# Scatters one a slot, the output projection ahead of the values, and the router slots' copy of the values moved to VectorE

## The chip, the cores and the metric

The kernel runs on one core of one Trainium2 chip. The metric is the device time of one execution, in microseconds (us). The kernel before has a median of 2207.32 us in three runs (2202.14 to 2223.04).

## The reference

The program computes four transformer layers on 32 sequences of 128 tokens with 256 features, in float32, each with a context of the same shape. Layer 0 projects queries, keys and values head by head, attends to the context with a key mask, and ends in a ReLU feed-forward. Layer 1 is a cross-attention with residual and layer norm. The next layer has a causal self-attention, a cross-attention, and a mixture of experts: a router picks 2 of 8 experts for each token. The last layer attends within a window, gates its result and normalises it. All attentions have 16 heads of 16 features:

```
scores = jnp.einsum('bqhd,bkhd->bhqk', Q, Kp) / jnp.sqrt(jnp.float32(HD))
a = jax.nn.softmax(scores, axis=-1)
o = jnp.einsum('bhqk,bkhd->bqhd', a, V).reshape(Bq, Sq, Dm)
return o @ wo + bo
...
topw, topi = jax.lax.top_k(router_weights, K)
h = jax.nn.gelu(jnp.einsum('td,edf->etf', xf, w1) + b1[:, None, :], approximate=False)
out = jnp.einsum('etd,te->td', eo, combine)
```

## The kernel before, in words

The program is written engine by engine, with semaphores between engines; each engine works through its own list in order. It has three phases. The first does the four attentions ahead of the experts, 128 of them, the second runs the experts over 72 tiles of 128 sorted tokens, the third does the last attention with its gate. The change touches the first phase alone.

The first phase is a chain of slots. A slot is one attention of one sequence. Four sequences go through layer 0, then the same four through layers 1, 2 and 3 (2 is the causal self-attention, 3 the cross-attention of the expert layer), so an iteration has 16 slots, numbered 0 to 15, with layer = slot // 4. There are 8 iterations. The first and the last are written out, the six between are one hardware loop on every engine, and their instructions carry register arithmetic for semaphore counts. `at_(d)` names the slot d places after the present one: `now` is d = 0, `prev` -1, `ff` -2, `rk_` -3, `nxt` +1, `nn` +2.

What each engine does in a slot of the light kind (slots 7 to 15 and 0 to 2; in slots 3 to 6 the feed-forward of layer 0 is mixed in):

- TensorE: scores of `now` (L861, in layer 2 with the mask's L828 ahead), keys and queries of `nxt` (L775, L809), the product of probabilities and values of `prev` (`av`, L926), the transposed maxima of `now` (L913), the transpose of the input of `nn` (L714, L729), the scores again, transposed and exact (`scores_t`, L881 and L888), the values of `nxt` (`values`, L793, or L787 for layer 0), and the output projection of `prev` (`wo`, L939). In slots 14, 15, 0 and 1, the router slots here, a transpose for the router (`fxt`, L714) ends the slot.
- VectorE: layer norm's statistics of `ff` (L1579 to L1584), row maxima of `now` (`mb`, L1557), the output of `prev` divided and transposed (`normalise`, L1567 to L1574, result `oT`), the low parts of queries and keys of `nxt` (`qk_lo`, L1542 or L1545), and the sum of projection and residual of `prev` (`yb`, L1719). In slot 2 it also copies the values of `nxt` from PSUM (`vz`, L1529), ahead of `qk_lo`.
- ScalarE: normalised rows (L1316), queries and keys out of PSUM (L1289, L1292), the transposed maxima (`mT`, L1296), the transposed inputs (L1274), four exponentials (`pt_all`, L1303), then the copy of the values (`vz`, L1375).
- GpSimd: root of the variance (L2030), scaled residuals (L2042, L2044), the queries expanded by heads (`expand`, L2007), then in slots 7 to 10 the scatter of a finished sequence's rows into the experts' order (L2050), then `expand_lo` (L2014).

An iteration's scatters are two indirect DMAs a sequence, one for each chosen expert. They go out in the next iteration: `routed(at_, 8 + s)` is true for sequence s in slot 7 + s. The positions they need are computed by VectorE in slot 6.

## Time and profile before

| what | us |
| --- | --- |
| median of three runs | 2207.32 |
| fastest and slowest run | 2202.14, 2223.04 |
| profiled execution | 2205.66 |
| its span in the trace | 2201.1 |
| TensorE busy | 1972.7 (90%) |
| VectorE busy | 1437.2 (65%) |
| ScalarE busy | 1219.0 (55%) |
| GpSimd busy | 1080.9 (49%) |

The first phase takes about 1340 us of the span. No engine is busy all the time in a slot, so the busy shares don't say what a slot waits for. The chain of waits and the timeline of single slots do.

### The profile page before, as it was taken

The numbers are of one execution on the slowest core, as the hardware profiler recorded it, in microseconds if no ns is written. First come the engines' busy times: TensorE is split into PE (matmuls) and PEld (weight loads), VectorE is DVE, ScalarE is ACT, GpSimd is POOL, SyncE is SP. The second block draws the span as 40 slices with busy tenths as digits, with TensorE's granted clock in tenths as the row PEclk, the third lists the DMA queues.
The fourth block names the chain that finished last, engine by engine and source line by source line (L and its number), as shares of the span: only waits on it lengthen the run. The fifth ranks groups of instructions, "written<-read, shape, count | busy, mean of one in ns | idle before, by whom it ended". The sixth has DMA issues, their size and how long they took to land.

```text
span 2201.1 us, 73195 instructions
## 1 busy us (share of the span) xinstructions
PE 1972.7 (90%) x26048; PEld 1667.3 (76%) x26049; DVE 1437.2 (65%) x3384; ACT 1219.0 (55%) x3083; POOL 1080.9 (49%) x1592
## 2 busy tenths in 40 slices
PE   5999988988988988988988995999999997799997
PEld 4877776866876876776876874899999997677775
DVE  3577676676676676676676685444544543688886
ACT  3366465465465465455455463566556553567775
POOL 3355464464465464465465474322222100788884
PEclk9999999999999999999999996999999998899999
DMA  8501001001001001001000041311112111222220
GB/s 188 183 2 39 8 22 39 8 22 39 8 21 39 8 21 39 8 21 39 8 21 22 2 136 51 117 57 60 59 58 60 38 41 50 62 70 69 68 67 26
DMA packets 97250, 104.38 MB, mean 47 GB/s; under 512 B 23936, under 2 KB 88192, under 8 KB 96896
## 3 DMA queue, kind: packets, MB, share of 16 engines
q1 hardware_dynamic: 87936, 75.96, 11.4%
q0 software_dynamic: 8704, 25.19, 3.7%
q8 instruction: 167, 2.74, 0.5%
q14 instruction: 59, 0.48, 0.1%
q10 hardware_dynamic: 384, 0.01, 0.0%
HBM read 64.68 MB, written 36.44 MB: 46 GB/s over the span
## 4 chain that ended last, share of the span: by engine, by line
PE 64%; DVE 15%; issue 10%; ACT 5%; POOL 3%; DVEq 0%; DMA 0%; ACTq 0%; POOLq 0%; another core or an unknown queue 0%; SPq 0%
PE ps_scores L1137 11%; PE ps_w L1150 9%; DVE mb L1557 8%; PE ps_scores L881 6%; PE ps_w L939 5%; PE ps_xv L714 4%; PE ps_xv L793 4%; PE ps_qk L809 3%; PE ps_qk L960 3%; PE ps_xv L960 3%; PE ps_o L926 2%; ACT pt_all L1303 2%; DVE st L1579 2%; PE ps_scores L888 2%; PE ps_qk L804 1%
## 5 line engine op out<-in xcount | busy, mean ns | idle before, releaser
L1557 DVE TENSOR_REDUCE mb<-ps_scores 128x16 bf16<-128x2048 f32 x160 | 365.6, 2285 | 67.0 <-PE ps_scores L861 66.6
L1303 ACT ACTIVATE pt_all<-ps_scores 128x512 f32<-128x512 f32 x512 | 264.4, 603 | 52.6 <-PE ps_scores L888 47.9
L2030 POOL TENSOR_TENSOR rstd<-ve,neghalf 128x1 f32<-128x1 f32 x192 | 106.8, 556 | 348.0 <-DVE ve L1583 331.7
L1137 PEld LDWEIGHTS ps_scores<-tiles,w_now 128*128 128x128 f32 x2272 | 267.2, 193 | 4.8 <-issue 1.8
L1137 PE MATMUL ps_scores<-tiles,w_now 128*128 128x128 f32 x2272 | 267.8, 277 | 1.2 <-DVE tiles L1850 1.2
L1401 ACT ACTIVATE tiles<-ps_scores,b1s 128x128 f32<-128x128 f32 x568 | 154.6, 384 | 198.0 <-PE ps_scores L1137 182.7
L1150 PE MATMUL ps_w<-w_split,g_split 128*128 x1136 | 219.3, 346 | 5.7 <-DVE g_split L1869 5.7
L2007 POOL TENSOR_TENSOR qbd_all<-qT,consts 128x512 fp32r<-128x512 f32 x160 | 166.4, 1040 | 94.5 <-ACT kT L1289 85.1
L2014 POOL TENSOR_TENSOR lower<-lower,consts 128x512 fp32r<-128x512 f32 x160 | 166.7, 1042 | 86.2 <-DVE lower L1545 43.3
L1150 PEld LDWEIGHTS ps_w<-w_split,g_split 128*128 128x128 f32 x1136 | 174.8, 190 | 30.5 <-issue 6.4
L1316 ACT ACTIVATE xn<-yb,nb,rstd 128x256 f32<-128x256 f32 x160 | 96.3, 602 | 180.9 <-POOL nb L2037 178.9
L926 PE MATMUL ps_o<-pt_all,vz 128*32 128x128 f32 x5120 | 179.8, 282 | 1.3 <-DVE arena L1707 0.8
L926 PEld LDWEIGHTS ps_o<-pt_all,vz 128*32 128x32 f32 x5120 | 134.4, 112 | 25.0 <-issue 14.5
L1860 DVE TENSOR_TENSOR tiles<-ps_w,tiles 128x256 f32<-128x256 f32 x71 | 30.2, 425 | 186.9 <-PE ps_w L1150 186.9
L1719 DVE TENSOR_TENSOR yb<-ps_w,xr 128x256 f32<-128x256 f32 x128 | 54.2, 424 | 141.2 <-PE ps_w L939 140.3
L1393 ACT COPY w_now<-w_experts 128x2048 f32 x72 | 140.2, 1948 | 9.9 <-issue 9.9
L2142 POOL DMA_INDIRECT arena<-sorted_y,pidx x64 | 63.7, 995 | 165.7 <-DMA sorted_y<-tiles 150.4
L2120 POOL CAST w_split<-w_raw 128x256 fp32r<-128x256 f32 x64 | 24.1, 421 | 243.8 <-DVE g_split L1869 238.6
L1274 ACT ACTIVATE xT<-ps_xv,cols_all 128x128 f32<-128x128 f32 x256 | 103.8, 457 | 59.2 <-PE ps_xv L714 58.5
L939 PE MATMUL ps_w<-arena,oT 128*128 128x256 f32 x512 | 133.7, 384 | 2.1 <-DVE oT L1574 2.1
L1567 DVE STREAM_TRANSPOSE ps_o<-ps_o 128x512 f32<-128x512 f32 x160 | 116.1, 725 | 21.6 <-PE ps_o L926 19.9
L714 PE MATMUL ps_xv<-consts,xn 128*128 128x128 f32 x384 | 80.6, 292 | 51.3 <-ACT vz L1375 15.1
(254 smaller groups left out, 4777.8 us busy)
## 6 DMA issues: line engine op xcount, KB each, us to landing
tiles<-sorted_x SPq DMA_DIRECT2D x72, 128.0 KB, 2.0
sorted_y<-tiles SPq DMA_DIRECT2D x71, 128.0 KB, 1.7
w_experts<-in_L_xattn_e_w SPq DMA_DIRECT2D x8, 1024.0 KB, 10.3
w_raw<-in_L_xattn_e_w POOLq DMA_DIRECT2D x8, 1024.0 KB
sorted_x<-zeros SPq DMA_DIRECT2D x8, 640.0 KB
ct_scratch<-cT SPq DMA_DIRECT2D x32, 128.0 KB, 1.7
x_scratch<-x2b_all SPq DMA_DIRECT2D x32, 128.0 KB, 1.7
arena<-x_scratch SPq DMA_DIRECT2D x32, 128.0 KB
```

What stands on the lines that cost most here:

```text
L714: last = nc.tensor.transpose(ps[:, P * c:P * (c + 1)], src[:, P * c:P * (c + 1)], ident)
L881: mm(ps_s[:, g, PAIR * P * c:PAIR * P * (c + 1)], k_[at_strip, kc, :].bitcast(F32R), q_[at_strip, c].rearrange("p e q -> p (e q)").bitcast ...
L926: last = mm(ps_o[32 * q:32 * q + 32, 2 * par + c, :], vz[p][:, h].rearrange("p a d -> p (a d)"), pt[:, SLOTS * q + PAIR * c + par, :], sta ...
L939: last = mm(ps_w[:, 0:D], oT[:, c, :], w[:, c, :], start=c == 0, stop=c == KC - 1)
L1137: last = mm(ps_s[:, 2 * par + j // 4, P * (j % 4):P * (j % 4 + 1)], w1_now[:, par, c, P * j:P * (j + 1)], xgT[par][:, c, :], start=c == 0, ...
L1150: return mm(ps_w[:, 0:n], g_split[:, g_, j, :].bitcast(F32R), w2_split[:, bass.ds(odd * (2 * FC * D) + j * 2 * D, n)].bitcast(F32R), start ...
L1303: nc.scalar.activation(pt[:, 4 * g:4 * g + 4, :].rearrange("p h q -> p (h q)"), ps_s[:, g, :], ACT.Exp, bias=bias, scale=LAYER[l]["scale"] ...
L1393: nc.scalar.copy(w1_now[:, par].rearrange("p c n -> p (c n)"), w1f[:, bass.ds(e * (KC * FF), KC * FF)]).then_inc(w1_copied, 1)
L1401: last = nc.scalar.activation(gT[:, j, :], ps_s[:, 2 * par + j // 4, P * (j % 4):P * (j % 4 + 1)], ACT.Gelu, bias=b1s[par][:, j:j + 1])
L1557: V.tensor_reduce(mb[:].rearrange("p (g r) -> p g r", g=BANKS)[:, :, 0:SLOTS], ps_s[:].rearrange("p g (h k) -> p g h k", h=SLOTS), AX_X, A ...
L2007: G.tensor_tensor(qbd[p].bitcast(F32R), qT[:].unsqueeze(2).to_broadcast([P, KC, PAIR, P]), hmask.unsqueeze(1).unsqueeze(3).to_broadcast([P ...
L2014: G.tensor_tensor(qbd_lo.bitcast(F32R), qT_lo.unsqueeze(2).to_broadcast([P, KC, PAIR, P]), hmask.unsqueeze(1).unsqueeze(3).to_broadcast([P ...
```

## The change

Three edits, all in the first phase.

1. TensorE: in light slots other than slot 2 `wo(prev)` is issued ahead of `values(nxt)` instead of behind it.
2. The copy of the values of `nxt` out of PSUM moves from ScalarE, where it stands behind the exponentials, to VectorE, where it stands ahead of `qk_lo`, in slots 14, 15, 0 and 1.
3. GpSimd: the eight scatters of an iteration go out one a slot in slots 6 to 13, instead of two a slot in slots 7 to 10. In the tail behind the last iteration they stay two a slot.

```diff
@@ TensorE, light slots
                 if now["ok"]:
                     scores_t(now)
+
+                wo_last = ff["ok"] and ff["l"] == 0
+                if prev["ok"] and not wo_last:
+                    wo(prev, first and tau - 1 == 0, w_free)
                 if nxt["ok"]:
...
                     values(nxt, nn["t"] + 1 if nn["ok"] and nn["l"] != 1 else nxt["t"] + 1)
-                if prev["ok"]:
+                if prev["ok"] and wo_last:
                     wo(prev, first and tau - 1 == 0, w_free)
@@ ScalarE
-                if nxt["ok"] and not ff_now:
+                if nxt["ok"] and not (ff["ok"] and ff["l"] in (0, LAYERS - 1)):
                     wait(act, v_psum, nxt["t"] + 1)
@@ VectorE
                 if nxt["ok"]:
-                    if ff["ok"] and ff["l"] == 0:
+                    if ff["ok"] and ff["l"] in (0, LAYERS - 1):
                         vz_evac(nxt)
@@ GpSimd
-        def scatter(n, s):
+        def scatter(n, s, choices=range(TOPK)):
...
-            for k_ in range(TOPK):
+            for k_ in choices:
...
-            for s in range(NS):
-                if routed(at_, 8 + s):
-                    if last and tau == TPI + 8 - 1:
-                        pool.wait_ge(tail_zeroed, 16 * E)
-                    scatter(routed(at_, 8 + s), s)
+
+            if last and tau >= TPI:
+                for s in range(NS):
+                    if routed(at_, 8 + s):
+                        if s == 0:
+                            pool.wait_ge(tail_zeroed, 16 * E)
+                        scatter(routed(at_, 8 + s), s)
+            else:
+                for i_ in range(NS * TOPK):
+                    if routed(at_, 7 + i_):
+                        scatter(routed(at_, 7 + i_), i_ // TOPK, (i_ % TOPK,))
```

The order of VectorE's instructions in slot 14 of the loop (a router slot), from the row maxima of that slot to those of the next. Before:

```order
L1557 TENSOR_REDUCE mb<-ps_scores 128x4x4
L1567 STREAM_TRANSPOSE ps_o<-ps_o 128x512
L1569 RECIPROCAL o_inv<-ps_o 128x16
L1571 TENSOR_TENSOR route_all<-ps_o,o_inv 128x2x8x16
L1574 STREAM_TRANSPOSE oT<-route_all 128x256
L99 REGISTER_ALU
L1545 SCALAR_TENSOR_TENSOR lower<-ps_qk,cols_all,qT 128x128 x2
L1545 SCALAR_TENSOR_TENSOR lower<-ps_qk,cols_all,kT 128x128 x2
L99 REGISTER_ALU
L1719 TENSOR_TENSOR yb<-ps_w,xr 128x256
```

With the change (its line numbers are 4 higher):

```order
L1561 TENSOR_REDUCE mb<-ps_scores 128x4x4
L1571 STREAM_TRANSPOSE ps_o<-ps_o 128x512
L1573 RECIPROCAL o_inv<-ps_o 128x16
L1575 TENSOR_TENSOR route_all<-ps_o,o_inv 128x2x8x16
L1578 STREAM_TRANSPOSE oT<-route_all 128x256
L99 REGISTER_ALU
L1533 COPY vz<-ps_xv 128x16x16
L1549 SCALAR_TENSOR_TENSOR lower<-ps_qk,cols_all,qT 128x128 x2
L1549 SCALAR_TENSOR_TENSOR lower<-ps_qk,cols_all,kT 128x128 x2
L99 REGISTER_ALU
L1723 TENSOR_TENSOR yb<-ps_w,xr 128x256
```

The copy of the values now stands between `oT` and `qk_lo`, and so ahead of `yb` too.

TensorE in a light slot of layer 2, one piece of the difference:

```order
 L881 MATMUL ps_scores<-qbd_all,lower 128x256 x4
 L888 MATMUL ps_scores<-mT,ecol_b 128x128 x16
+L939 MATMUL ps_w<-arena,oT 128x256 x2
 L793 MATMUL ps_xv<-arena,xT 128x256 x2
-L939 MATMUL ps_w<-arena,oT 128x256 x2
 L828 MATMUL ps_scores<-ident_b,route_all 128x4x32 x16
```

The projection moved ahead of the two matmuls of the values; the next slot's scores follow as before.

GpSimd in a slot with scatters, in the loop. Before, and then with the change:

```order
L2007 TENSOR_TENSOR qbd_all<-qT,consts 128x512
L2050 DMA sorted_x<-x2b_all,posu 34688x256 x2
L99 REGISTER_ALU
L2014 TENSOR_TENSOR lower<-lower,consts 128x512
L99 ISA
```

```order
L2011 TENSOR_TENSOR qbd_all<-qT,consts 128x512
L2054 DMA sorted_x<-x2b_all,posu 34688x256
L99 REGISTER_ALU
L2018 TENSOR_TENSOR lower<-lower,consts 128x512
L99 ISA
```

One scatter is left in the slot, at the same place behind `expand`, and there are eight such slots where there were four.

## Rows read from the trace of the kernel before

**Rows 1.** The page, part 4: the chain that ended last, by engine.

```profile
PE 64%; DVE 15%; issue 10%; ACT 5%; POOL 3%; DVEq 0%; DMA 0%; ACTq 0%; POOLq 0%; another core or an unknown queue 0%; SPq 0%
```

**Rows 2.** Chain of waits, slot 13 in the loop: start us, us, what.

```profile
655.64 2.21 DVE mb L1557
...
659.86 1.06 PE ps_xv L793 x4
660.92 0.88 PE ps_w L939 x4
...
661.92 0.44 DVE yb L1719
```

**Rows 3.** Timeline, slot 13: start, us, engine, line, form, count [idle before <-releaser].

```profile
654.13 0.41 PE L861 MATMUL ps_scores<-kT,qbd_all 32*128 32x128 bf16 x16 [0.22 <-ACT pt_all L1303]
...
659.26 0.45 DVE L1574 STREAM_TRANSPOSE oT<-route_all 128x256 f32<-128x256 f32 x1
...
659.46 0.40 PE L888 MATMUL ps_scores<-mT,ecol_b 32*128 32x128 bf16 x16
...
659.89 2.06 ACT L1303 ACTIVATE pt_all<-ps_scores 128x512 f32<-128x512 f32 x4 [0.34 <-PE ps_scores L888]
...
662.01 0.41 PE L861 MATMUL ps_scores<-kT,qbd_all 32*128 32x128 bf16 x16 [0.23 <-ACT pt_all L1303]
```

**Rows 4.** Timeline, first iteration (no loop, no scatters): slots 8, 9, 12 and 13.

```profile
124.33 2.28 DVE L1557 TENSOR_REDUCE mb<-ps_scores 128x16 bf16<-128x2048 f32 x1
...
132.12 2.28 DVE L1557 TENSOR_REDUCE mb<-ps_scores 128x16 bf16<-128x2048 f32 x1
...
155.51 2.28 DVE L1557 TENSOR_REDUCE mb<-ps_scores 128x16 bf16<-128x2048 f32 x1
...
162.88 2.28 DVE L1557 TENSOR_REDUCE mb<-ps_scores 128x16 bf16<-128x2048 f32 x1
```

**Rows 5.** Timeline, slots 8 and 9 in the loop, with scatters.

```profile
611.29 0.40 PE L828 MATMUL ps_scores<-ident_b,route_all 32*128 32x128 bf16 x16 [0.23 <-ACT pt_all L1303]
...
616.92 0.40 PE L888 MATMUL ps_scores<-mT,ecol_b 32*128 32x128 bf16 x16
...
617.23 1.05 POOL L2050 DMA_INDIRECT sorted_x<-x2b_all,posu  x1 [0.17 <-issue]
...
617.82 2.06 ACT L1303 ACTIVATE pt_all<-ps_scores 128x512 f32<-128x512 f32 x4 [0.99 <-PE ps_scores L888]
...
627.35 2.06 ACT L1303 ACTIVATE pt_all<-ps_scores 128x512 f32<-128x512 f32 x4 [1.66 <-PE ps_scores L888]
```

**Rows 6.** Timeline, slot 8 of the last iteration: exponentials and scatter.

```profile
1283.44 2.06 ACT L1303 ACTIVATE pt_all<-ps_scores 128x512 f32<-128x512 f32 x4 [0.72 <-PE ps_scores L888]
1283.53 1.05 POOL L2050 DMA_INDIRECT sorted_x<-x2b_all,posu  x1 [0.17 <-issue]
```

**Rows 7.** Timeline, slot 14 in the loop, a router slot.

```profile
667.98 1.13 PE L793 MATMUL ps_xv<-arena,cT 128*128 128x256 f32 x4
...
670.01 0.40 ACT L1375 COPY vz<-ps_xv 128x256 f32<-128x256 f32 x1
670.11 0.42 DVE L1719 TENSOR_TENSOR yb<-ps_w,xr 128x256 f32<-128x256 f32 x1 [1.52 <-PE ps_w L939]
...
671.86 2.28 DVE L1557 TENSOR_REDUCE mb<-ps_scores 128x16 bf16<-128x2048 f32 x1
```

**Rows 8.** Timeline, slot 2, where VectorE copies the values already.

```profile
705.60 0.42 DVE L1529 COPY vz<-ps_xv 128x256 f32<-128x256 f32 x1 [0.50 <-PE ps_xv L787]
...
706.66 0.41 DVE L1719 TENSOR_TENSOR yb<-ps_w,xr 128x256 f32<-128x256 f32 x1
```

**Rows 9.** Timeline, slot 0 behind the loop's back edge.

```profile
682.63 0.91 PE L804 MATMUL ps_qk<-xT,arena 128*128 128x128 f32 x4 [2.10 <-issue]
...
688.42 0.71 PE L787 MATMUL ps_xv<-arena,cT 128*128 128x128 f32 x4
...
692.36 2.29 DVE L1557 TENSOR_REDUCE mb<-ps_scores 128x16 bf16<-128x2048 f32 x1 [0.54 <-PE ps_scores L861]
```

## The prediction

> **What bounds the kernel now.** I read the page first, then the chain of waits, then the timeline slot by slot. The chain that ended last is TensorE for 64% and VectorE for 15% [rows 1], and busy shares don't say which of the two a slot waits for. The chain of one light slot in the loop does [rows 2]: the row maxima `mb` take 2.21 us, the exact scores follow, then the values (1.06 us), then the output projection (0.88 us), then VectorE's sum `yb`, layer norm's statistics, and the next `mb`. So `mb` waits not for its scores but for VectorE's own list, in which the statistics stand ahead of it; these wait for the projection, and that stands behind the values. Meanwhile the scores that `mb` reads began at 662.01 [rows 3]; the `mb` of that slot began at 663.43, which is 1.4 us later, though the scores are 0.41 us long. About 0.9 us of slack lies on the scores' side.
>
> How short can such a slot get? I measure a light slot from one `mb` to the next. The first iteration runs the same slots without the loop's register instructions and without scatters: a causal slot takes 132.12 - 124.33 = 7.79 us, a plain one 162.88 - 155.51 = 7.37 [rows 4]. The loop has 662.01 - 654.13 = 7.88 for the plain one [rows 3]. TensorE, with its scores, keys, queries, `av` and exact scores, and ScalarE, which moves queries and keys out ahead of the maxima, have little room below that, so I take 7.79 and 7.37 as floors.
>
> **Edit 1, the projection ahead of the values.** No instruction is added or removed; two groups of 0.9 to 1.1 us change places. In slots 8 to 13 `wo` comes about 1 us earlier, so the statistics no longer bind, until the floor does. From the scores of slot 8 at 611.29 to those of slot 14 at 662.01 the loop takes 50.72 us [rows 3, 5]. At the floors, four causal and two plain slots take 4 x 7.79 + 2 x 7.37 = 45.90. The gain is 4.8 us an iteration, if no scatter disturbs, and 6 x 4.8 = 28.9 us in the six iterations of the loop. It is not 1 us a slot in all light slots: past half a microsecond in the plain ones the engines just named take over, and `oT`, ready 659.26 + 0.45 = 659.71, would then make `wo` wait 0.1 or 0.2 us. The first and last iterations stand at the floor already: 0. What could be hurt is the values' copy, late by 0.9 us; ScalarE reaches it only behind its exponentials (659.89 + 2.06 = 661.95 in slot 13), which covers all but 0.1 to 0.2 us, and `av` needs it only over 2 us later. Nothing.
>
> **Edit 3, the scatters.** The number of scatters, their bytes and the 1.05 us of GpSimd for each stay; each light slot of GpSimd has room for one. What a scatter does to others is in the rows. Without one the exponentials start 659.89 - 659.46 = 0.43 us after the last score group [rows 3]. In slot 8, where a scatter starts 0.31 us into that group, they start 617.82 - 616.92 = 0.90 us after it, and their idle time is 0.99 us; in slot 9 it is 1.66, 0.67 more [rows 5]. So a scatter that starts as the last scores run delays their signal by 0.47 us, and once by 1.14. In the last iteration the scatter starts 0.09 us after the exponentials have begun [rows 6] and they are not delayed. The bounds for one scatter are 0 and 1.14 us. Before, the slots 8 to 10 pay this largely under cover of the late statistics. After the change nothing covers it: exponentials that start later make the next scores later, and the slot sits at its floor. GpSimd gets to its scatter by a chain from the statistics (root, normalised rows, two residuals, `expand`) which shifts with `mb`, while the exact scores come 0.5 us earlier, so the scatter still starts within half a microsecond of the last scores. I take 0.5 us, nearest to slot 8, in six slots (8 to 13), since slot 7 has the same start as before and slot 6 has over 1 us of cover in its feed-forward: 6 x 6 x 0.5 = +18 us, with the ends 0 and 6 x 6 x 1.14 = +41.
>
> Sentences on a page, which the sum does not need: the Trainium skill (SBUF — State Buffer, "Who interferes with whom") says that only the port pair shared by VectorE and GpSimd causes contention and that "PE and ACT never wait on anyone". By it a scatter could not delay TensorE's signal to ScalarE. The rows of slot 8 speak against it, with 0.47 us, so I go by the rows; what the rule would give is the first rival.
>
> **Edit 2, the values' copy in the router slots.** ScalarE is relieved of 0.40 us that no chain of these slots needs much: the router's transpose on TensorE waits for the copy and comes 0.1 us later to 0.4 us earlier. VectorE's list gets a wait. The copy stands ahead of `qk_lo` and of `yb`, and it waits for the values, which edit 1 has just moved back by 0.9 us. Behind it are queued `qk_lo`, `yb`, the statistics and the next `mb`. The price of that queue is shown by slot 2: from the copy to `yb` 706.66 - 705.60 = 1.06 us [rows 8], and about 0.3 more where keys and queries have biases (slot 14).
>
> - Slot 14. Before, `yb` starts at 670.11 and `mb` 1.75 us later, at 671.86 [rows 7]; `qk_lo` had been done long before. Now, with the slot 0.5 us earlier, `wo` starts near 667.5, the values 0.9 later at 668.4, the copy after their 1.13 us at 669.6, `yb` 1.4 later at 671.0, `mb` at 672.8. Loss 0.95 us. Where edit 1 brings nothing (first and last iteration) it is 1.4. In all 6 x 1.0 + 2 x 1.4 = 8.8.
> - Slot 0. `mb` waited for its scores (idle 0.54 until L861) at 692.36. Now the values start not at 688.42 but at 689.7, the copy at 690.5, `yb` at 691.6 and `mb` 1.6 later at 693.2. Loss 0.9 [rows 9], five times; the two iterations with other starts lose 0.8 together: 5.3.
> - Slot 1, by the same construction, 0.6 us six times and 0.3 once: 3.9. An estimate; its rows are as those of slot 0.
> - Slot 15. VectorE is late by the same 0.6 us, but behind the loop's back edge TensorE stands still for 2.10 us and starts its next work at 682.63 [rows 9], after which `mb` is long done. That covers it, and the transpose for the router comes 0.2 us earlier: -0.7 over all.
>
> Together +17.3 us.
>
> **The sum.** -28.9 + 18.0 + 17.3 = +6.4 us. On the profiled execution's 2205.66 that is 2212.1. This execution lies 1.7 us under the median of the runs (2207.32), well within their spread of 21; I take 2213.
>
> **Rivals.**
> - *No delay by scatters* (what the skill's rule gives). For: in the last iteration there is none, and the new start could slip behind the last scores everywhere. Against: slots 8, 9 and 10 of the loop show it in every iteration, and the scatter's start moves with the same chain. Then -28.9 + 17.3 = -11.6: 2195 us. Chance 0.16.
> - *No loss in the router slots*: the copy's wait stays under the scores' side. For: in slots 15, 0 and 1 `mb` waits for scores today. Against: the working above, and slot 2, where `yb` follows at the queue's pace. Then -28.9 + 18 = -11: 2196 us. Chance 0.11. Both of these at once: -28.9, 2178 us, chance 0.05.
> - *Slower*: each of the eight scatters holds TensorE's signals as in slot 9. Place: between the last exact scores and the exponentials of slots 8 to 13. Price 1.14 us: +41 instead of +18, so +29: 2236 us. For: slots with causal mask send the signal about 0.3 us later after the scatter's start than now, into its middle. Against: two of three such slots show 0.47. It gets to 1% from 0.93 us a scatter on. Chance 0.14.
> - *The swap does not reach the floor*, since the loop's register instructions hold these slots at, say, half the way: -14 instead of -29: 2227 us. Chance 0.10.
>
> The forecast itself has the rest, 0.44, with its own range of 2204 to 2222.
>
> **How the numbers follow.** A change within 1% (22 us) can't be told from none with runs that spread like these. Faster by over 1%: the double rival and a little of the first two, 0.08. Slower by over 1%: most of the slow rival and a part of the last, 0.16. Within 1%: 0.76. The range that should hold 8 in 10 leaves out the double rival and the upper end of the slow one: 2186 to 2236.
>
> **What would show it.** After the change: in slot 13 `mb` starts 0.7 to 0.8 us after its scores instead of 1.4, and the slot is 7.4 to 8.0 long. ScalarE's idle time ahead of the exponentials is over 0.8 us in slots 8 to 13. In slots 14, 0 and 1 the copy on VectorE has an idle time of 1 us or more ahead of it, with the values as its releaser, and `mb` follows `yb` with no idle time; slot 14 is 10 us long against 8.4. An iteration of the loop stays within 2 us of its present length. I am wrong if slots 11 to 13 get no longer by their new scatter, if `mb` in the router slots still waits for scores, or if the time behind the back edge moves by more than 1 us an iteration.

## The result, and the profile after

The changed kernel takes 2235.87 us in the median of four runs (2232.06 to 2236.84), the kernel before 2208.95 in the median of four (2202.14 to 2223.04). The ratio is 1.011, with a 95% interval of 1.0059 to 1.0162: slower by 1.1%. The profiled execution took 2236.78 us, its span is 2234.9. The forecast was 2213 in a range of 2186 to 2236; the time lies 0.13 us inside the upper end of that range, where the slower rival stood.

From the first `mb` to the last of the first phase the changed kernel needs 32.1 us more; the rest of the program, which no edit touches, differs by 2 us. Measured from one `mb` to the next, and taken over the six iterations of the loop, the 32.1 us are made of: slots 8 to 13 together +2.8, slot 14 +11.6, slot 6 +7.7, slot 7 +2.8, slot 15 +1.8, slots 0 and 1 -0.5 together, the first iteration +0.3, the last +5.7.

The page of the changed kernel, part 4 and one group of part 5:

```profile
PE 65%; DVE 12%; issue 10%; ACT 7%; POOL 3%; DMA 0%; DVEq 0%; ACTq 0%; POOLq 0%; another core or an unknown queue 0%
...
L1307 ACT ACTIVATE pt_all<-ps_scores 128x512 f32<-128x512 f32 x512 | 263.8, 603 | 95.1 <-PE ps_scores L888 89.9
```

The chain hardly differs from [rows 1]. The idle time ahead of the exponentials, 89.9 of it put down to the last exact scores, is 95.1 us over the run. On the page of before that group had 52.6 us. This is the first hint of where the time went: not into a longer operation, but between TensorE's scores and ScalarE.

Timeline of the changed kernel, slot 13, which answers to [rows 3] (start, us, engine, line, form, count, idle time and releaser):

```profile
665.70 2.29 DVE L1561 TENSOR_REDUCE mb<-ps_scores 128x16 bf16<-128x2048 f32 x1 [0.43 <-PE ps_scores L861]
...
669.98 0.40 PE L888 MATMUL ps_scores<-mT,ecol_b 32*128 32x128 bf16 x16
670.10 1.05 POOL L2054 DMA_INDIRECT sorted_x<-x2b_all,posu  x1 [0.17 <-issue]
...
670.81 1.13 PE L939 MATMUL ps_w<-arena,oT 128*128 128x256 f32 x4 [0.43 <-DVE oT L1578]
...
671.49 2.06 ACT L1307 ACTIVATE pt_all<-ps_scores 128x512 f32<-128x512 f32 x4 [1.61 <-PE ps_scores L888]
...
672.07 0.42 DVE L1723 TENSOR_TENSOR yb<-ps_w,xr 128x256 f32<-128x256 f32 x1 [0.31 <-PE ps_w L939]
...
673.61 0.41 PE L861 MATMUL ps_scores<-kT,qbd_all 32*128 32x128 bf16 x16 [0.81 <-ACT pt_all L1307]
...
674.07 2.29 DVE L1561 TENSOR_REDUCE mb<-ps_scores 128x16 bf16<-128x2048 f32 x1 [0.41 <-PE ps_scores L861]
```

The swap does what I said: `wo` starts at 670.81 and `yb` at 672.07, and `mb` no longer stands behind the statistics; it has an idle time of 0.41 us and waits for its scores. But the exponentials start 1.51 us after the last score group (671.49 - 669.98), where the kernel before had 0.43. The scatter starts 0.12 us into that group and ends at 671.15; the exponentials start 0.34 us after its end. The slot is 674.07 - 665.70 = 8.37 us long. I had expected 7.4 plus 0.5.

Timeline of the changed kernel, slot 8 with its scatter, which answers to [rows 5]:

```profile
627.40 1.05 POOL L2054 DMA_INDIRECT sorted_x<-x2b_all,posu  x1 [0.17 <-issue]
...
627.46 0.41 PE L888 MATMUL ps_scores<-mT,ecol_b 32*128 32x128 bf16 x16
...
628.83 2.06 ACT L1307 ACTIVATE pt_all<-ps_scores 128x512 f32<-128x512 f32 x4 [1.65 <-PE ps_scores L888]
```

Here too the exponentials come 1.37 us after the last scores. All of the slots 8 to 13 look like one of these two: 8.63, 8.64, 8.65, 8.40, 8.39 and 8.37 us long.

Timeline of the changed kernel, slot 6, the first with a scatter now:

```profile
610.88 1.08 POOL L2054 DMA_INDIRECT sorted_x<-x2b_all,posu  x1 [0.17 <-issue]
...
611.26 1.82 DVE L1665 TENSOR_TENSOR w_all<-ew,wt 128x4 f32 x1
...
611.99 1.05 POOL L2018 TENSOR_TENSOR lower<-lower,consts 128x512 fp32r<-128x512 f32 x1
...
613.00 0.41 DVE L1723 TENSOR_TENSOR yb<-ps_w,xr 128x256 f32<-128x256 f32 x1
...
614.49 2.28 DVE L1561 TENSOR_REDUCE mb<-ps_scores 128x16 bf16<-128x2048 f32 x1
```

And the same place before:

```profile
602.24 1.04 POOL L2014 TENSOR_TENSOR lower<-lower,consts 128x512 fp32r<-128x512 f32 x1
...
603.22 0.15 DVE L1661 TENSOR_TENSOR w_all<-ew,wt 128x4 f32 x1
```

The product `w_all` of 128x4 elements takes 1.82 us instead of 0.15. It lasts from the middle of the scatter to the end of `expand_lo`. `yb` and `mb` queue behind it: slot 6 is 1.29 us longer in each iteration.

TensorE waits for that late `mb` at the start of slot 7, 1.55 us ahead of L913 where the kernel before has 0.26. Later in slot 7 its granted clock falls to 0.5 (1.2 GHz) for a while, in all six iterations of the loop; in the kernel before it stays at 1.00 (2.4 GHz) there. In slot 15, at whose start TensorE waits 1.65 us instead of 0.60, it falls in two of the first five iterations. Windows from `mb` to `mb` of slot 7, then of slot 15 with and without the fall (window, its length, busy time and count of PE, PEld, DVE, ACT and POOL, granted clock, DMA share, GB/s):

```profile
614.49:623.00 8.51, 6.82 (x116) 5.02 (x109) 6.31 (x16) 5.24 (x13) 5.39 (x8) 0.80 0.05 17
...
513.32:523.40 10.08, 6.85 (x107) 5.09 (x99) 6.34 (x18) 4.91 (x12) 4.92 (x7) 0.83 0.09 29
684.46:693.08 8.62, 5.39 (x107) 3.94 (x99) 6.34 (x18) 4.91 (x12) 4.92 (x7) 1.00 0.11 34
```

Slot 15 with the fall is 1.46 us longer than without it, for the same work. At the full clock it takes 8.62 us, less than the 8.72 to 8.81 of the kernel before. The +1.8 of slot 15 is thus the clock's, and so is a large part of slot 7; the first group of experiments gives its price there.

Timeline of the changed kernel, slot 14, which answers to [rows 7]:

```profile
681.21 0.42 DVE L1533 COPY vz<-ps_xv 128x256 f32<-128x256 f32 x1 [2.09 <-PE ps_xv L793]
...
682.58 0.42 DVE L1723 TENSOR_TENSOR yb<-ps_w,xr 128x256 f32<-128x256 f32 x1
...
684.46 2.28 DVE L1561 TENSOR_REDUCE mb<-ps_scores 128x16 bf16<-128x2048 f32 x1
```

The copy waits 2.09 us for the values, `yb` starts 1.37 us after the copy and `mb` 1.88 after `yb`. `mb` to `mb` this slot takes 10.38 us in the mean of the loop; before it took 8.45.

### The profile page after: what moved, and what is told of

Read it like the earlier page. It is cut to its first block, busy times and chain, and to the rows that moved or that the text cites. A ratio compares the mean times of both kernels' runs of the same rounds, so it can differ in the third digit from the quotient of the medians.

```text
span 2234.9 us, 73247 instructions
## 1 busy us (share of the span) xinstructions
PE 1976.1 (88%) x26048; PEld 1671.1 (75%) x26049; DVE 1461.4 (65%) x3413; ACT 1213.9 (54%) x3054; POOL 1083.9 (48%) x1592
## 4 chain that ended last, share of the span: by engine, by line
PE 65%; DVE 12%; issue 10%; ACT 7%; POOL 3%; DMA 0%; DVEq 0%; ACTq 0%; POOLq 0%; another core or an unknown queue 0%
PE ps_scores L1141 11%; PE ps_w L1154 9%; DVE mb L1561 6%; PE ps_scores L881 5%; PE ps_qk L809 5%; ACT pt_all L1307 4%; PE ps_w L939 4%; PE ps_o L926 4%; PE ps_qk L775 4%; PE ps_scores L888 3%; PE ps_xv L714 3%; PE ps_qk L960 3%; PE ps_xv L960 2%; PE ps_xv L793 2%; PE ps_scores L828 2%
## 5 line engine op out<-in xcount | busy, mean ns | idle before, releaser
L1307 ACT ACTIVATE pt_all<-ps_scores 128x512 f32<-128x512 f32 x512 | 263.8, 603 | 95.1 <-PE ps_scores L888 89.9
L939 PE MATMUL ps_w<-arena,oT 128*128 128x256 f32 x512 | 147.7, 413 | 18.9 <-DVE oT L1578 18.9
L939 PEld LDWEIGHTS ps_w<-arena,oT 128*128 128x128 f32 x512 | 91.3, 197 | 41.4 <-DVE oT L1578 29.9
L973 PE MATMUL ps_w<-arena 128*128 128x256 f32 x512 | 119.1, 386 | 0.0
```

The costliest lines, as they stand in the source:

```text
L939: last = mm(ps_w[:, 0:D], oT[:, c, :], w[:, c, :], start=c == 0, stop=c == KC - 1)
L973: last = mm(ps_w[:, 0:D], hT[:, j, :], w_ff2[:, j, :], start=j == 0, stop=j == FC - 1)
L1307: nc.scalar.activation(pt[:, 4 * g:4 * g + 4, :].rearrange("p h q -> p (h q)"), ps_s[:, g, :], ACT.Exp, bias=bias, scale=LAYER[l]["scale"] ...
```

## The experiments

Twelve kernels ran in three groups of four, each group on a chip of its own with the kernel before beside it. That matters here. In the first and the third group the kernel before took 2184.80 and 2184.84 us, in the second 2205.59, as in the runs of the result (2208.95). So ratios are read within a group.

### First group: each edit alone, and a gated scatter

**Edit 1 alone.** The diff is edit 1 of the change and nothing else.

> Edit 1 alone: the projection ahead of the values, the scatters two a slot in slots 7 to 10, the values' copy on ScalarE. Theory (a scatter that is running while the last exact scores finish holds TensorE's signal for 0.9 to 1.1 us, and edit 1 moved those scores into it): slots 11 to 13 at 7.6, 7.5 and 7.4 us, slots 8 to 10 near 8.6 each, slots 14 to 1 no longer than before; in all 8 to 15 us faster than the kernel before (about 2195 us). Rival (the prediction's 0.5 us a scatter): slots 8 to 10 at 8.3, about 2190 us. Rival (the swap itself costs): slots 11 to 13 no shorter than 7.9, no gain.

2163.68 us against 2184.80, ratio 0.990 (0.9884 to 0.9917). Slot 13 of it:

```profile
642.30 0.40 PE L888 MATMUL ps_scores<-mT,ecol_b 32*128 32x128 bf16 x16
...
642.74 2.06 ACT L1306 ACTIVATE pt_all<-ps_scores 128x512 f32<-128x512 f32 x4 [0.34 <-PE ps_scores L888]
...
645.89 2.28 DVE L1560 TENSOR_REDUCE mb<-ps_scores 128x16 bf16<-128x2048 f32 x1
```

The exponentials start 0.44 us after the last scores, and the slot is 7.50 us long. Slots 8 to 13 sum to 46.12 us, where I had put the floor at 45.90. The mechanism and the floor of edit 1 are right where nothing disturbs it; its gain on this chip is 21.1 us, and it comes not from slots 8 to 13 alone, for slot 7 is 7.16 us long and slot 14 8.07, where the kernel before has 8.06 and 8.45 in its trace, which is from another group. That its pairs of scatters disturb nothing I first put down to their start, since in slots 8 and 9 it lies after the signal; the third group shows that this was not the whole reason. Slot 8:

```profile
604.67 2.06 ACT L1306 ACTIVATE pt_all<-ps_scores 128x512 f32<-128x512 f32 x4 [0.72 <-PE ps_scores L888]
604.74 1.05 POOL L2053 DMA_INDIRECT sorted_x<-x2b_all,posu  x1 [0.17 <-issue]
```

**Edit 3 alone.** The diff is edit 3 of the change and nothing else.

> Edit 3 alone: scatters one a slot in slots 6 to 13. Theory: slot 6 is 1.3 us longer, because VectorE's small product of two SBUF operands is blocked by GpSimd; slots 8 to 10 get shorter since a second scatter no longer meets the projection's signal; slots 11 to 13 get a few tenths longer, mostly under cover of the late statistics. Together within 8 us of the kernel before (2200 to 2215 us). Rival (each scatter costs a slot 0.5 us or more whatever the order of the projection): 8 x 0.5 x 6 less what slots 7 to 10 save, 10 us slower or more.

2191.97 us, ratio 1.0028 (1.0014 to 1.0041). Slot 6 pays 1.29 us here as well, so that loss belongs to edit 3 by itself. Slot 8:

```profile
614.17 0.40 PE L888 MATMUL ps_scores<-mT,ecol_b 32*128 32x128 bf16 x16
614.48 1.05 POOL L2050 DMA_INDIRECT sorted_x<-x2b_all,posu  x1 [0.17 <-issue]
...
614.68 1.08 ACT L1303 ACTIVATE pt_all<-ps_scores 128x512 f32<-128x512 f32 x2 [0.60 <-PE ps_scores L888]
```

The scatter starts 0.31 us behind the start of the last score group, exactly as in slot 8 of [rows 5], but the exponentials start 0.51 us behind that start and not 0.90. The same overlap costs 0.1 us here and 0.5 there. In slot 12 the scatter starts 0.07 us after the exponentials, and they come 0.43 us after the scores.

This trace also gives the price of the clock in slot 7, whose `mb` is as late as in the changed kernel. The granted clock falls in three of the six iterations, and the slot takes 9.39 to 9.53 us with the fall and 7.86 to 7.88 without it:

```profile
600.55:610.07 9.52, 7.87 (x125) 6.04 (x118) 6.22 (x16) 5.09 (x13) 5.31 (x7) 0.82 0.04 15
767.29:775.16 7.87, 5.99 (x122) 4.65 (x115) 6.22 (x16) 5.03 (x13) 5.32 (x7) 1.00 0.05 19
```

**Edits 1 and 2.**

```diff
+                if prev["ok"] and not wo_last:
+                    wo(prev, first and tau - 1 == 0, w_free)
...
-                    if ff["ok"] and ff["l"] == 0:
+                    if ff["ok"] and ff["l"] in (0, LAYERS - 1):
                         vz_evac(nxt)
```

> Edits 1 and 2: projection first, the router slots' values' copy on VectorE, scatters as before. Theory: against edit 1 alone slot 14 is 1.5 to 2 us longer, slots 15, 0 and 1 change by less than 0.5 us each; 12 to 18 us slower than edit 1 alone. Rival (the copy is not what makes slot 14 long, but the scatters ahead of it): within 5 us of edit 1 alone.

2182.21 us, ratio 0.998 (0.996 to 0.9999): 18.5 us over edit 1 alone on the same chip. Slot 14 is 10.01 us long instead of 8.07, slot 15 10.28 instead of 9.24, slot 1 0.26 longer, slot 0 0.3 shorter. The size is the one forecast for edit 2 (17.3), but it falls in slots 14 and 15, not in 0 and 1. Slot 15's part is the clock again: its granted clock falls in four of the first five iterations, which take 10.03 to 10.20 us, and the one without a fall takes 8.62.

**Edit 1, and pairs of scatters behind a wait for the last scores.**

```diff
+                    if nxt["ok"]:
+                        wait(pool, st_ready, 4 * nxt["t"])
                     scatter(routed(at_, 8 + s), s)
```

> Edit 1 with the scatters two a slot in slots 7 to 10 as before, but each pair waits on GpSimd until TensorE's last exact scores of the slot have signalled. Theory (the signal is held only when a scatter runs as it is sent): the exponentials start as early as without scatters, slots 8 to 10 at 7.8 to 8.3 us and slots 7 to 13 at the floors; about 25 us faster than the kernel before (2180 us). Rival (a running scatter holds every signal of TensorE, wherever it stands): the projection's signal is held instead, statistics late, slots 8 to 10 at 8.5 us or more, no faster than edit 1 alone.

2183.19 us, ratio 0.9997 (0.9978 to 1.0017). The first theory missed; the rival had the size but not the cause, for no signal was held. Slot 10:

```profile
629.24 0.41 PE L888 MATMUL ps_scores<-mT,ecol_b 32*128 32x128 bf16 x16
...
629.67 2.06 ACT L1306 ACTIVATE pt_all<-ps_scores 128x512 f32<-128x512 f32 x4 [0.78 <-PE ps_scores L888]
...
630.68 1.05 POOL L2053 DMA_INDIRECT sorted_x<-x2b_all,posu  x1 [1.09 <-PE ps_scores L888]
...
632.04 0.96 POOL L2053 DMA_INDIRECT sorted_x<-x2b_all,posu  x1 [0.30 <-issue]
```

The gate opened 1.09 us before the first scatter started, and the pair ended at 633.00. `expand_lo` behind it ended only at 634.07, and so the root of the variance began 1.54 us after the next `mb` (634.02 against 632.48; with edit 1 alone it is 0.35 in slot 11). The normalised rows waited for it (634.96), ScalarE's queries, keys and transposed maxima queued behind them (`mT` at 636.47), and the exact scores waited for these. Slots 8 to 11 are 8.71, 8.81, 8.34 and 8.44 us long without any held signal. The wait had moved further down GpSimd's own queue.

### Second group: where the scatter stands

**Edits 1 and 3 without 2**, that is, the changed kernel with the copies as before.

> Edits 1 and 3 without 2. Edit 1 alone took 21 us off (ratio 0.990), edit 3 alone added 6 us. Theory (the two edits meet: the projection ahead of the values makes the exact scores end 0.1 to 0.4 us later after the start of the scatter, and a single scatter that begins as they run holds their signal to ScalarE until it is done): the exponentials of slots 8 to 13 start 5.8 to 5.9 us after mb instead of 4.9, these slots are 8.3 to 8.7 us long instead of 7.4 to 8.1, and with slot 6 (+1.3 us) the kernel is 5 to 12 us slower than before. Rival (the edits add up): 21 less and 6 more, 15 us faster than before, ratio 0.993, slots 8 to 13 at 7.4 to 8.1.

2216.27 us against 2205.59, ratio 1.004 (1.0012 to 1.0068). Slot 13:

```profile
660.35 0.40 PE L888 MATMUL ps_scores<-mT,ecol_b 32*128 32x128 bf16 x16
660.46 1.05 POOL L2053 DMA_INDIRECT sorted_x<-x2b_all,posu  x1 [0.17 <-issue]
...
661.83 2.06 ACT L1306 ACTIVATE pt_all<-ps_scores 128x512 f32<-128x512 f32 x4 [1.59 <-PE ps_scores L888]
```

Held as in the changed kernel: 1.48 us instead of 0.43. Slots 8 to 13 sum to 50.86 us, against 51.08 in the changed kernel and 50.61 in the kernel before. The time is the theory's, and edit 2 is no part of the hold. Slot 7 is 7.30 us long here against 8.52 in the changed kernel: `mb` is as late and TensorE waits 1.54 us, but the granted clock stays at 1.00 in all six iterations. By this comparison the clock cost the changed kernel about 1.2 us an iteration in slot 7, some 7 us in all; why it fell in one kernel and not in the other is open. Whether edit 1 alone would be held on this chip is not known, since it ran on others; so that the hold costs this is shown, that it takes both edits is not.

**The single scatter behind `expand_lo`.**

```diff
+            if nxt["ok"]:
+                expand_lo(nxt)
             if not (last and tau >= TPI):
                 for i_ in range(NS * TOPK):
                     if routed(at_, 7 + i_):
                         scatter(routed(at_, 7 + i_), i_ // TOPK, (i_ % TOPK,))
-            if nxt["ok"]:
-                expand_lo(nxt)
```

> Edits 1 and 3 without 2, and the single scatter stands behind expand_lo in GpSimd's list instead of ahead of it, so that it starts after the exact scores are done. Theory (the overlap of scatter and last scores is what costs): no signal is held, exponentials 4.9 us after mb, slots 8 to 13 within 0.2 us of edit 1 alone (7.4 to 8.1), in all 15 to 24 us faster than before. Rival (a scatter costs its slot about as much wherever it stands, through GpSimd's chain to the next root and residuals): 8.3 us slots, within 5 us of the kernel with edits 1 and 3 alone.

2188.12 us, ratio 0.9908 (0.9881 to 0.9935): 28 us below the kernel with the same edits and the scatter ahead of `expand_lo`, on the same chip. Same scatters, same bytes, one place further back. Of the 28 us, 7.7 are slot 6's and 18 those of slots 8 to 13: slot 6 is at 13.71 again, the exponentials start on time, and slots 8 to 13 sum to 47.85 against 50.86. That is still 1.7 us above edit 1 alone, and the start of slot 13 shows why:

```profile
643.91 0.41 PE L861 MATMUL ps_scores<-kT,qbd_all 32*128 32x128 bf16 x16 [0.22 <-ACT pt_all L1306]
643.98 1.05 POOL L2053 DMA_INDIRECT sorted_x<-x2b_all,posu  x1 [0.17 <-issue]
...
645.29 2.29 DVE L1560 TENSOR_REDUCE mb<-ps_scores 128x16 bf16<-128x2048 f32 x1 [0.73 <-PE ps_scores L861]
```

Now it is the next scores that are held: they should be done at 644.32, the scatter ends at 645.03, `mb` starts at 645.29. My expectation "no signal is held" was wrong for this edge.

**An ordinary operation in the scatter's old place**, with the scatter where the last kernel has it.

```diff
+            if any(routed(at_, 7 + i_) for i_ in range(NS * TOPK)) and not (last and tau >= TPI):
+                G.tensor_tensor(spare[:].rearrange("p (a b c) -> p a b c", a=KC, b=PAIR), qT[:].unsqueeze(2).to_broadcast([P, KC, PAIR, P]),
+                                hmask.unsqueeze(1).unsqueeze(3).to_broadcast([P, KC, PAIR, P]), ALU.mult)
             if nxt["ok"]:
                 expand_lo(nxt)
```

> As the kernel with the scatter behind expand_lo, but where the scatter stood an ordinary GpSimd operation of the same length (a product of 128x512 into a spare tile, about 1.04 us, nothing uses it) is added in slots 6 to 13. Theory (it is the indirect DMA that holds TensorE's signal): the exponentials still start at 4.9 us after mb, slots 8 to 13 stay within 0.2 us of the kernel without the added operation. Rival (any busy GpSimd, or the later expand_lo, does it): exponentials at 5.8 us, slots of 8.3 to 8.7 us, about 25 us slower than without the operation.

2190.31 us, ratio 0.9921 (0.9892 to 0.9949), 2 us from the kernel without the operation, within the intervals. Slot 13:

```profile
648.59 1.04 POOL L2102 TENSOR_TENSOR spare<-qT,consts 128x512 bf16<-128x512 f32 x1
...
648.65 0.40 PE L889 MATMUL ps_scores<-mT,ecol_b 32*128 32x128 bf16 x16
...
649.08 2.06 ACT L1307 ACTIVATE pt_all<-ps_scores 128x512 f32<-128x512 f32 x4 [0.34 <-PE ps_scores L889]
```

GpSimd is busy with an operation of 1.04 us at the very moment at which the scatter did harm, and the exponentials start 0.43 us after the scores. It is the indirect DMA that holds the signal, not a busy GpSimd.

**Edits 1 and 2, with the copy behind `yb`**, and pairs of scatters as before the change.

```diff
                 if nxt["ok"]:
                     if ff["ok"] and ff["l"] == 0:
                         vz_evac(nxt)
...
                 if prev["ok"]:
                     residual_sum()
+                if nxt["ok"] and ff["ok"] and ff["l"] == LAYERS - 1:
+                    vz_evac(nxt)
```

> Edit 1 and edit 2, the copy of the values standing behind yb in VectorE's list in slots 14, 15, 0 and 1 instead of ahead of qk_lo. Edits 1 and 2 as made gave 18.5 us more than edit 1 alone. Theory (the cost is the queue behind the copy's wait: yb, the statistics and the next mb): slot 14 loses 0.3 us against edit 1 alone instead of 1.9, slots 15, 0 and 1 lose under 0.3, in all 14 to 22 us faster than before. Rival (the copy costs wherever it stands on VectorE, since mb is then 0.42 us later, or av waits for vz): 1 us or more in slot 14, in all 8 us or less faster than before.

2188.33 us, ratio 0.9922 (0.989 to 0.9953). Slot 14 is 8.39 us long, slot 15 8.90, slot 1 7.68, slot 0 11.28. So the cost of edit 2 was the queue behind the copy's wait; behind `yb` the copy on VectorE gains in slots 0, 1 and 15. But its slots 8 to 13 sum to 50.98, no less than in the kernel before (50.61): with pairs of scatters, edit 1 gains nothing there on this chip. Falls of the granted clock behind the longest waits add to it (slot 11 takes 9.24 to 9.40 us with them and 7.80 without). Slot 10, with its pair of scatters:

```profile
627.29 1.05 POOL L2055 DMA_INDIRECT sorted_x<-x2b_all,posu  x1 [0.17 <-issue]
...
627.35 0.41 PE L888 MATMUL ps_scores<-mT,ecol_b 32*128 32x128 bf16 x16
...
628.64 0.96 POOL L2055 DMA_INDIRECT sorted_x<-x2b_all,posu  x1 [0.30 <-issue]
...
630.07 2.06 ACT L1306 ACTIVATE pt_all<-ps_scores 128x512 f32<-128x512 f32 x4 [3.00 <-remote]
```

The exponentials start 2.72 us after the last scores, behind both scatters.

### Third group: the mended kernels

**One gated scatter a slot**, in slots 7 to 14, with edit 1.

```diff
+                for i_ in range(NS * TOPK):
+                    if routed(at_, 8 + i_):
+                        wait(pool, st_ready, 4 * nxt["t"])
+                        scatter(routed(at_, 8 + i_), i_ // TOPK, (i_ % TOPK,))
             if nxt["ok"]:
                 expand_lo(nxt)
```

> Edit 1, and one scatter a slot in slots 7 to 14, ahead of expand_lo, behind a wait for the signal of the last exact scores; no edit 2. Slot 6 has no scatter. Theory (a running scatter holds TensorE's signals; the one stretch in which none is awaited lies between the last scores' and the projection's, from mb + 4.4 to mb + 5.9 us, and a gated scatter just fits): exponentials at mb + 4.4 to 4.7 us, mb with under 0.3 us of idle time, causal slots 7.8 to 8.0 us and plain ones 7.5, 24 to 32 us faster than before (ratio 0.985 to 0.989). Rival (as with the gated pairs, expand_lo behind the scatter comes late for the next exact scores): slots of 8.3 us and more, ratio 0.995 to 1.0.

2158.81 us against 2184.84, ratio 0.9884 (0.9867 to 0.9901). Slot 12:

```profile
633.91 2.07 ACT L1306 ACTIVATE pt_all<-ps_scores 128x512 f32<-128x512 f32 x4 [0.37 <-PE ps_scores L888]
...
634.92 1.05 POOL L2053 DMA_INDIRECT sorted_x<-x2b_all,posu  x1 [1.05 <-PE ps_scores L888]
...
636.00 1.05 POOL L2017 TENSOR_TENSOR lower<-lower,consts 128x512 fp32r<-128x512 f32 x1
...
637.09 2.28 DVE L1560 TENSOR_REDUCE mb<-ps_scores 128x16 bf16<-128x2048 f32 x1
```

The scatter starts 1.01 us behind the exponentials, `expand_lo` still ends before the next `mb`, and slots 8 to 13 sum to 46.03.

**The same with edit 2, the copy behind `yb`.**

> As the gated scatters, one a slot in slots 7 to 14, and edit 2 with the copy behind yb. Theory (the three edits are worth having once no scatter lies on a signal and no yb stands behind the copy's wait): slots 0 and 1 are 0.6 to 1.1 us shorter than with edit 1 alone, slot 14 0.3 longer, slot 15 0.3 shorter, so 8 to 12 us below the gated kernel: 34 to 42 us faster than before, ratio 0.981 to 0.985. Rival (the gain of slots 0 and 1 comes from the alignment of that one profile): no difference to the gated kernel beyond 4 us.

2145.69 us, ratio 0.9821 (0.9804 to 0.9838), faster than the kernel before by 1.8% and than each other kernel of this group. Slots 0, 1 and 15 are 11.46, 7.68 and 8.84 us long, with edit 1 alone 12.07, 8.31 and 9.27. Part of slot 0 is the clock, which falls behind every back edge and for lengths that vary; in the first iteration of the loop, which has no back edge ahead of it and the full clock, slot 0 takes 7.73 us against 8.42. The three edits are all in it, the second and the third in other places than in the changed kernel.

**Edit 1 alone again.**

> Edit 1 alone again, on the same chip as the gated kernels. Theory: 0.990 as the first time, 4 to 10 us above the gated kernel, since pairs of scatters hold a signal now and then. Rival: level with the gated kernel or below it.

2163.73 us, ratio 0.9911 (0.9896 to 0.9926), as the first time. The gated kernel lies 4.9 us below it. The two profiles don't show that difference (their spans are 2155.2 and 2154.6 us), so I call it unexplained; that pairs now and then hold a signal was not seen.

**The changed kernel with the scatter behind `expand_lo`.**

> The changed kernel with one thing altered: the single scatter stands behind expand_lo. Theory: the hold of the last scores' signal was worth 27 us of it and slot 6 another 8, so it is 28 to 36 us faster than the changed kernel: at most 4 us from before, ratio 0.995 to 1.0, with edit 2 still costing its 18. Rival (with the copy on VectorE the slots are bound there, and the scatter's place matters less): within 10 us of the changed kernel, ratio above 1.005.

2182.70 us, ratio 0.9993 (0.998 to 1.0006). Against the changed kernel's 1.011 this would be some 26 us, but that ratio was taken on another chip, and the trace shows that the place of the scatter is not all of it. Start of slot 9:

```profile
615.71 0.40 PE L861 MATMUL ps_scores<-kT,qbd_all 32*128 32x128 bf16 x16
615.82 1.05 POOL L2054 DMA_INDIRECT sorted_x<-x2b_all,posu  x1 [0.17 <-issue]
...
616.27 2.28 DVE L1561 TENSOR_REDUCE mb<-ps_scores 128x16 bf16<-128x2048 f32 x1
```

The scores end in the middle of the scatter, and `mb` starts before the scatter has ended. In the second group such a signal was held by 0.7 to 0.9 us.

**Which chips hold.** Over all fourteen traces I compared when TensorE's signals fell due after the start of a scatter with when they came, by the times of the semaphores' updates. In the kernels of the first and third group the delay is never above 0.33 us, mostly none. In the traces of before and after, and in all four of the second group, 485 of the 523 signals due 0.2 to 0.8 us after the start come 0.6 us or more late, mostly by 0.6 to 1.2 us and by more behind pairs. The exceptions are in slots 6 to 10, most of them signals of the values, the projection and a transpose. Slot 6 is the cleanest pair: in the kernel with the scatter behind `expand_lo` and in the changed kernel altered in the same way, the instructions around are the same and the scores' signals fall due some 0.2 us into the scatter; they come 1.1 us late in the second group and at once in the third. (`mb` stands behind the statistics there and loses nothing by it.) Slot 8 of edit 3 alone against [rows 5], shown above, is the same comparison with a price. With the kernel before itself 21 us slower in the second group than in the other two, the chip is the likeliest cause. It stays open what differs between the chips, whether it is the chip or only the session on it, and neither the changed kernel nor edit 1 alone was run on a chip of each kind.

## Why the prediction was right, and where it was not

The sum said +6.4 us, the first phase shows +32.1. The sign and most mechanisms held, the sizes did not all. That the range held the time is luck: the median lies 0.13 us inside its end, and two of the four runs, 2236.78 and 2236.84, lie outside. The likeliest outcome, within 1% with 0.76, did not come; slower by over 1% had 0.16, and the interval of 0.6 to 1.6% leaves both open.

Of the signs that I had named, the idle time ahead of the exponentials came (1.6 us), and so did the copy's wait for the values in slots 14, 15, 0 and 1 (2.09, 1.83, 1.67 and 1.75 us, with `mb` right behind the statistics) and a slot 14 of 10 us. A slot 13 of 7.4 to 8.0 us did not (8.37), and an iteration grew by 4.3 us, not by less than 2.

- **Edit 1, the floor right, the gain counted too high.** Forecast: floor 45.90 us for slots 8 to 13. Measured without holds: 46.12 and 46.13, in the gated kernel 46.03. `mb` behind its scores, as stated. But the 28.9 us were counted from slots 8 to 10 of [rows 5], which take 8.81, 9.18 and 8.79 us where slot 11 without a scatter takes 8.07: up to 15 us of the gain are held signals of the pairs, and where signals are held edit 1 does not take them away. Beside the kernel before on one chip it gained 21.1 us, and by its trace a part of this lies in slots 7 and 14, which the sum left at nothing.
- **Edit 3 in slots 8 to 13, the step that failed in size.** Forecast 0.5 us a slot, taken "nearest to slot 8". Measured on the chip of the second group: (50.86 - 46.12) / 6 = 0.79 us a slot (the two sums from chips of the two kinds), in the changed kernel (51.08 - 46.12) / 6 = 0.83. The exponentials are late by 0.9 to 1.1 us in all six slots. Against 18 us this makes 30 in the loop, and slots 8 to 13 of the last iteration, which I had left out, add 4.8. What I read wrongly in [rows 5] is which of its rows the new slots resemble. In slot 8 of before the scatter starts 0.31 us behind the start of the last score group; in the changed kernel that is 0.12 us in slot 13, and in slot 8 the scatter starts 0.06 us ahead of the group. The signal falls due deeper in the scatter, as the slower rival argued, and is held until its end. Slot 9 of before, which I kept for the end of the range, was the nearer row. The slower rival had mechanism and place; its price of 1.14 was too high for a slot's length.
- **Slots 6 and 7, missed.** I costed them at nothing and named over 1 us of cover in slot 6. The cover was there for TensorE, not for VectorE's `w_all`, which GpSimd blocked: +7.7 us, shown in three kernels with the scatter in that place and absent in every kernel without. The page that I set against slot 8 has the half of this case that is `expand_lo` (the Trainium skill, SBUF — State Buffer, "Who interferes with whom"): a VectorE instruction with two inputs in SBUF contends with a GpSimd instruction that reads SBUF. Here the trace agrees: the product ends 0.04 us after `expand_lo`. The scatter blocks it too, for the product, begun 0.38 us into the scatter, was not done at its end 0.70 us later, where it takes 0.15 us alone.
- **TensorE's clock, a term put at nothing.** Slot 7 added 2.8 us net: edit 1 alone makes it 0.9 us shorter an iteration (by traces of different groups), the fall of the clock behind the late `mb` makes it some 1.2 us longer. Slot 15 lost 1.5 us in each of the two iterations with a fall. The loop of the changed kernel runs 53 us at 1.2 GHz, that of the kernel before 31. In slot 7 and in the first half of slot 15 a fall came only in iterations in which TensorE had waited 1.5 us or more at the start of the slot, but not in each of these; what decides is open.
- **Edit 2, the queue right, the places wrong.** Forecast +17.3; measured on one chip 18.5. Slot 14 became 1.94 us longer in the loop, twice my 0.95. Half a microsecond of that is an error of my books: I took the loss against the old time of the next `mb` with slot 13 already 0.5 us shorter, a gain that edit 1 had been credited with. The other half is `wo`, which waits for `oT` and starts 5.10 us after `mb` (679.17 against 674.07), where I had 4.57. Slot 15 lost 1.0 us an iteration under edits 1 and 2, but that is the clock: at the full clock it is 8.62 us long against 8.72 to 8.81 before, so the copy costs nothing there, and the forecast's -0.7 over all was right but for the clock. Slots 0 and 1 lost 0.2 us an iteration, where I had 0.9 and 0.6: at the full clock slot 0 takes 8.64 us against 8.42, slot 1 8.53 to 8.58 against 8.31. That slot 0 shows a gain over the loop goes with its clock, at 1.2 GHz for 24 us there instead of 31. That edit 2 measured 18.5 against 17.3 is therefore luck: some 12 us are slot 14's queue, some 6 the clock in slot 15.
- **The sentence on the skill.** That same section says that "PE and ACT never wait on anyone". In slot 13 TensorE's last scores ran on time beside the scatter. What came late were its signals, and only on some chips: the exponentials of slot 13 (1.51 us behind the scores instead of 0.43) speak against the rule for the kernel's purposes, slot 8 of edit 3 alone (0.51 us) is nearly as the rule says. By that the rival "no delay by scatters" fits the chips of two groups out of three.
- **The range.** It held the time only because the slow rival was let in: three misses of one sign (+12 and +5 from the holds, +10 from slots 6 and 7) make up the distance from the forecast.

## What to carry to other kernels

A stage that is relieved by a swap takes its time from the next wait in line, so look first at what runs beside that wait; here a one-microsecond indirect DMA of an engine with half its time free decided about a percent. Place such an operation by the signals that are awaited while it runs, not by the free time of its own engine. And a copy that waits for a late result belongs behind the work of its queue that is needed sooner: the same copy cost 18 us ahead of `yb` (on one chip, with pairs of scatters, a third of it by the clock) and gained 13 behind it (on another, with gated ones). And compare slots at the same granted clock, before a difference is put down to the queue.

## What was not expected of the hardware

- A TensorE signal that falls due while GpSimd issues an indirect DMA came up to 1.2 us late, 0.2 to 0.4 us after the end of the scatter, and 2.3 us late with two scatters in a row. An ordinary GpSimd operation of the same length did nothing. This showed in one of three groups and in the traces of before and after; the kernel before is 21 us slower in that group than in the others (2205.59 against 2184.8).
- VectorE's product of two small SBUF operands, begun in the middle of a scatter, ended only with the GpSimd operation behind the scatter (1.82 us). The copy just ahead of it, with one operand, took 0.17 us beside the scatter and 0.61 beside an ordinary GpSimd operation.
- A scatter behind a wait started 1.05 to 1.09 us after the signal that it waited for.
- A wait of TensorE of 1.5 to 1.7 us at the start of a slot was followed by a granted clock of 0.5 in some iterations and not in others of the same loop; it cost 1.4 to 1.7 us a time where one trace has both.
